# Layer 1's attention on one Trainium2 core: low parts of the turned probabilities ahead of the next head's maxima on VectorE

## What is computed

```python
qkv = x @ w_attn + b_attn                      # x: the conditioned input, (4, 512, 512)
att = einsum('bhqd,bhkd->bhqk', q, k) * scale  # 16 heads of 32
att = softmax(where(causal, att, -inf))
y   = einsum('bhqk,bhkd->bhqd', att, v)
x   = x + (y @ w_proj + b_proj)
```

## Time and profile before

| | us |
|---|---|
| median of three runs | 2220.79 |
| the profiled execution, its own time | 2226.78 |
| its span | 2225.1 |
| TensorE matmuls busy in the span | 1925.1 |
| VectorE busy in the span | 1565.3 |
| ScalarE busy in the span | 1392.1 |

### The profile page before, as it was taken

How to read it: one execution, slowest core, us unless ns; L and a number is a source line. 1 busy time by engine, 2 the same in 40 slices (tenths; PEclk the granted TensorE clock), 3 DMA queues, 4 the chain that set the end, 5 groups by cost and what they waited for, 6 DMA issues and landing times. The chain is left out here.

```text
span 2225.1 us, 40195 instructions
## 1 busy us (share of the span) xinstructions
PE 1925.1 (87%) x14497; PEld 1195.8 (54%) x14497; DVE 1565.3 (70%) x3486; ACT 1392.1 (63%) x3343; POOL 1146.9 (52%) x890
## 2 busy tenths in 40 slices
PE   0789999999999999999995699856898888878999
PEld 0445555656666666556563355434556566633444
DVE  7668788788888887777742499646677777743770
ACT  6588886777767776777743244236768686745442
POOL 5788886776776676566532366433323222200540
PEclk9889999999999999999987799968899999889999
DMA  4334332222223213343214844364434343435100
GB/s 172 125 98 142 112 107 70 91 98 74 89 76 92 88 58 103 121 127 120 74 39 170 327 146 147 126 233 136 134 100 135 94 145 112 142 123 171 41 34 19
DMA packets 110977, 256.72 MB, mean 115 GB/s; under 512 B 10944, under 2 KB 39744, under 8 KB 108736
## 3 DMA queue, kind: packets, MB, share of 16 engines
q1 hardware_dynamic: 91520, 204.92, 27.8%
q10 hardware_dynamic: 16704, 40.90, 5.2%
q0 software_dynamic: 2560, 8.39, 1.0%
HBM read 175.79 MB, written 75.24 MB: 113 GB/s over the span
## 5 line engine op out<-in xcount | busy, mean ns | idle before, releaser
L1001 PE MATMUL ps_q<-a_y,a_w 128*128 128x512 f16 x1536 | 344.3, 381 | 57.3 <-POOL a_y L701 57.3
L1001 PEld LDWEIGHTS ps_q<-a_y,a_w 128*128 128x128 f16 x1536 | 148.1, 98 | 225.3 <-issue 60.5
L724 POOL TENSOR_TENSOR a_rb<-a_rb,router_y 128x512 f32<-128x512 f32 x128 | 167.6, 1309 | 136.9 <-ACT a_rb L863 136.7
L1215 DVE TENSOR_REDUCE a_nmax<-ps_s 128x1 f32<-128x512 f32 (+3 forms) x256 | 123.6, 483 | 144.7 <-PE ps_s L1022 144.2
L1048 PE MATMUL ps_o<-a_tt_,a_v 128*128 128x512 f32 (+3 forms) x512 | 164.3, 467 | 36.9 <-ACT a_tt_ L905 34.3
L862 ACT ACTIVATE a_rb<-ps_q 64x512 f32<-64x512 f32 x128 | 76.1, 594 | 170.4 <-DVE a_ra L1200 168.6
L1010 PE MATMUL ps_v<-a_w,a_y 128*128 128x128 f16 x3072 | 182.6, 219 | 0.0
L1010 PEld LDWEIGHTS ps_v<-a_w,a_y 128*128 128x128 f16 x3072 | 174.9, 98 | 1.2
L1070 PE MATMUL ps_v<-a_o,a_wo 128*128 128x512 f16 x732 | 169.7, 382 | 1.9 <-ACT a_v L889 1.9
L882 ACT ACTIVATE ps_s<-ps_s,a_nmax 128x512 f32<-128x512 f32 (+3 forms) x256 | 125.3, 489 | 47.4 <-DVE a_nmax L1217 47.2
L733 POOL TENSOR_TENSOR a_q<-a_q 128x512 f16<-128x512 f32 x64 | 74.5, 1165 | 132.8 <-ACT a_q L896 132.8
(11 more groups left out here) (320 smaller groups left out, 4999.5 us busy)
## 6 DMA issues: line engine op xcount, KB each, us to landing
a_w<-wqkv_split SPq DMA_DIRECT2D x48, 768.0 KB, 4.6
scratch_numlog<-wkv_nl ACTq DMA_DIRECT2D x40, 512.0 KB, 2.7
wkv_kt<-in_fT ACTq DMA_DIRECT2D x56, 256.0 KB, 2.8
router_y<-in_wqkv SPq DMA_DIRECT2D x16, 768.0 KB, 5.4
wqkv_split<-a_w SPq DMA_DIRECT2D x16, 768.0 KB, 7.0
a_stacks<-qk_parts SPq DMA_DIRECT2D x96, 128.0 KB, 2.6
gate_up<-in_gate_up SPq DMA_DIRECT2D x8, 1408.0 KB, 11.4
a_nlc<-scratch_numlog SPq DMA_DIRECT2D x18, 512.0 KB, 4.9
```

What stands on the lines that cost most here:

```text
L724: pool.tensor_tensor(rb[:, n, :], rb[:, n, :], rot[:, 2 * n + 1, :], ALU.mult).then_inc(s["roped"], 1)
L1001: mm = pe.matmul(psq[n][:], w16[:, g % 2, wp, n, c, :], y16[b % 2][:, yp, c, :], start=c + m == 0, stop=c == CC - 1 and m == 2)
L1215: dve.tensor_reduce(nmax[:, 0, j:j + 1], cols(ps, j), AX, ALU.max, negate=True)
```

## The change

On VectorE the low parts of head h are called ahead of the maxima of head h+1 (and so also ahead of the moved rows and of the second piece of the output projection, which follow the maxima). No instruction is added or taken away, and the other engines' programs stay as they are.

```diff
                             more = not final(b) or q + 1 < CC
+                            turned_low(h, i)
                             if more or i + 1 < HPC:
                                 maxima(h + 1, i + 1)
                             if first and 0 < h <= 2 * TT:
                                 add_moved(2 * TT + h - 1)
                             if last_output:
                                 output(b - 1, 1)
-                            turned_low(h, i)
                             if last_output:
                                 output(b - 1, 2)
                             if i or q or not first:
```

## The result

The changed kernel takes 2328.89 us (2327.62 to 2331.82, four runs), against 2222.97 us of the kernel before, run beside it: a ratio of 1.0474, 95% interval [1.0433, 1.0514], 106 us slower. A second set of runs gave 1.0472 [1.0457, 1.0486]. The forecast was 68 us slower, 2289 with a range up to 2320: the direction was right, the size too small, and the measured time lies 9 us above the range.

The account below looks back on a forecast made before the run. Bound taken as a loop of maxima, exponentials, ScalarE's pieces and VectorE's next piece, with low parts beside it. Terms 31.9 + 21.3 + 16.9 - 2.0 = 68.1 us on 2220.8 gave 2288.9 us, range 2250 to 2320.

Parts of the forecast that it names:

- 2.0 taken back: TensorE's 3.61 us wait for stacked operands: some of it hidden in a longer chunk, -2.0 us (0 to -3.6).
- the first batch's term: First batch's heads 1 to 8: moved rows and exponentials come later, 8 x 1.7 + 3.3 = 16.9 us slower.
- that of the output projection: Three heads with the output projection: 2.9 for heads 0 to 2 plus TensorE's 4.2 stop, 3 x 7.1 = 21.3 us.
- the ordinary chunks' term: Eleven ordinary chunks: late exponentials in heads 0 and 1 delay each by 2.9 us, 31.9 us in all.
- as this is part of TensorE's loop I count it once, 3.3: First batch: `values` waits longer for moved rows, behind low parts (1.62) and maxima (1.67); counted once, 3.3 us.
- 8 x 1.7: First batch's heads 1 to 8: ScalarE's exponentials start about 1.7 us later in each head.
- The high end of 27.2: First batch, upper bound: all of 1.62 + 0.1 + 1.67 in each head, 8 x 3.4 = 27.2 us.
- the replay: One ordinary chunk worked through step by step in the new order: 2.9 us later, head 0's copies already done.
- order does not change its sum: Ordinary chunks, heads 2 and 3: VectorE is its own bound, so nothing is added and the 2.9 is handed on.
- priced this wait at 0.3: Ordinary chunks, head 3: a wait of some 0.3 us for the copies, only in the high bound of 3.5.
- The faster one: Rival: TensorE's 26.3 us of waits for low parts vanish and nothing else is late, 2194.5 us; chance 0.05.
- The clock's rival: Rival: more waits slow TensorE's clock in one head of each of 16 chunks, 22 us more, 2311; chance 0.15.

## Why the prediction was wrong in size

The time line tells where the 106 us lie. The first `turn` of layer 1, `ot_low` of head 9 and the last `ot_low`, first in the kernel before and then in the changed one:

```profile
1497.08 2.27 PE L2333 MATMUL ps<-ident,a_ef 128*128 128x128 f32 x10
...
1581.22 0.69 DVE L2510 TENSOR_TENSOR a_ot<-ps_p,a_ot 128x512 f16<-128x512 f32 x1 [4.58 <-ACT a_ot L2129]
...
1965.84 0.69 DVE L2510 TENSOR_TENSOR a_ot<-ps_p,a_ot 128x512 f16<-128x512 f32 x1 [1.90 <-ACT a_ot L2269]
```
```profile
1493.55 1.98 PE L2333 MATMUL ps<-ident,a_ef 128*128 128x128 f32 x10
...
1613.39 0.69 DVE L2510 TENSOR_TENSOR a_ot<-ps_p,a_ot 128x512 f16<-128x512 f32 x1 [7.96 <-ACT a_ot L2129]
...
2066.76 0.69 DVE L2510 TENSOR_TENSOR a_ot<-ps_p,a_ot 128x512 f16<-128x512 f32 x1 [1.90 <-ACT a_ot L2269]
```

From the first to the second, the heads with the moved rows, it is 84.1 us before and 119.8 after: 35.7 longer, where the sum had 16.9. Behind these, the three chunks with an output projection are 29.1 us longer (21.3 in the sum) and the others 39.7 (31.9, less 2.0 taken back). Together that is 104.5. These are single executions: in kernels that leave a part as it was, the first part lies within 2.6 us of the kernel before, the second within 1.7 and the last up to 10.5 above it. So the first batch's term is clearly the one that was furthest off and that of the output projection is clearly short, while it is less sure that the ordinary chunks' term was too small.

**First batch: the step "as this is part of TensorE's loop I count it once, 3.3" failed.** The wait recurs in each head, because `values` stands ahead of the projection, the next scores and the next `turn` on the same engine, and the low parts of the next head wait for that `turn`. The run with late moved rows alone is 26 us slower, 3.3 in each of eight heads. That this is just the 1.62 + 1.67 of the forecast is chance: in that run no maxima stand between, and the row grew by 16.0, or 2.0 a head. What makes 26 of 16 was not taken apart; slow products behind the longer stops are a candidate. The other half of the term, 8 x 1.7, fits what is left. The high end of 27.2 replaced the 1.7 by the 3.4 instead of adding them; both in each head are 40, about what was measured.

**Heads with the output projection: the wait was right (3.94 against 4.2), the price was not.** The clock was put apart, as a rival with one `turn` and its scores in a chunk; here it falls on twelve products of 512 columns right behind the stop, 1.4 to 2.6 us more in each of the three heads. Where these heads alone were changed, the trace shows 18.9 us for them against 3 x 4.2 = 12.6 in the sum, and the slow second pieces (6.5) are what is missing.

**Ordinary chunks, heads 0 and 1: right in sum, partly by luck.** 14 chunks at 2.9 are 40.6, measured 41 for these heads alone. In the chunk shown the waits it named have about the lengths it gave. But the low parts of head 0 had to wait for their copies, by 1.1 to 1.2 us in six of 13 chunks and 3.1 in one, which the replay had at nothing; and the chunks lost between 0.6 and 4.8 us each.

**Ordinary chunks, heads 2 and 3: the step "order does not change its sum" failed.** It holds for VectorE's own work, not for the readiness of its inputs. In head 3 VectorE comes to the low parts ahead of ScalarE's copies, and the maxima had filled that time. I had priced this wait at 0.3, and only at the high end; it is 0.8 to 1.3 us with both heads moved and 1.5 to 2.6 with head 3 alone. In head 2 of the last batch ScalarE has a piece that I had overlooked. Alone these heads cost 20 us. In the whole change the ordinary chunks lose 39.7 us by the time line; heads 0 and 1 alone are 31.7 there, heads 2 and 3 alone 19.5, so the parts overlap.

**The 2.0 taken back** did not come: TensorE's longest such wait, 3.61 us, is 4.08 after.

```profile
1799.08 0.60 PE L2321 MATMUL ps<-a_stacks 96*128 96x512 f16 x1 [4.08 <-issue]
```

**The rivals.** The faster one fell on its own test: TensorE's wait for low parts went from 26.3 to only 22.5, and one of 24.6 for exponentials came behind it. So the rule of the Trainium skill that was weighed there ("Perfetto Trace Analysis", section Optimization Strategy), taken for one of the two inputs that the engine waits for, gave the wrong sign here. The clock's rival was right in kind: the granted clock fell from 0.92 to 0.84. The run in which TensorE was kept busy agrees with the Trainium skill ("TensorE: Matmul & The Clock Gate", section HAM oscillation), by which idle gaps between bursts of matmuls bring the slow clock back: without the gap the next products were granted 1.00. What the clock costs over the whole stretch was not measured; only the three places with the fill were.

## What to carry to other kernels

When two groups of work swap places on one engine, ask of each what else it waits for and what waits for it, also in the first and last pass, where the queues differ; a group that can fill the wait of the other belongs ahead of it. A wait that recurs on an in-order engine is counted once for each pass if the next pass's start hangs on it, and what a wait on the trace is worth is not known until its removal has been tried: 9.4 us less of one gave nothing that could be measured here. And where a stop of about 4 us falls ahead of a dense run of products on TensorE, as here, price the products behind it at the slow clock too, not only the stop.

## What was not expected of the hardware

After a stop of 3.94 us twelve products of 512 columns took 5.30, 4.33 and 4.43 us in three places, and 2.76 in all three when 16 unused products stood in the stop and left it 0.49 us long. Unused work on an engine thus made the changed kernel 7.5 us faster.

Behind shorter stops it can go either way, in the same place of the same kernel. Two executions of the changed kernel, the `turn` of one head, which takes 1.25 us at the full clock:

```profile
1872.82 1.31 PE L2333 MATMUL ps<-ident,a_ef 128*128 128x128 f32 x10 [1.80 <-ACT a_ef L2135]
```
```profile
1881.87 2.40 PE L2333 MATMUL ps<-ident,a_ef 128*128 128x128 f32 x10 [1.81 <-ACT a_ef L2135]
```

TensorE had done the same work ahead of both, at a granted clock of 1.00; in the `turn` it was 1.00 in the one and 0.50 in the other. What decides this was not found, so a single trace does not give the price of such a stop.
